# Feed-forward experts of a decoder layer: three batches sorted by expert on chip and computed in tiles of 256 rows, the fourth computed densely

## The chip, the cores and the metric

One core of one Trainium2 chip. The metric is the device time of one execution in microseconds (us); the kernel before has a median of 324.4 us over three runs (324.27 to 324.47).

## The reference, cut to what matters

```python
x = x + self_attention(layernorm(x))                 # B=4, S=256, D=128; 16 heads of 64
x = x + cross_attention(layernorm(x), ctx)           # 16 heads of 8
# the part that changes: x is (4, 256, 128), 8 experts, hidden 512, top 2
n = layernorm(x)
scores = n @ Wr + br
_, topk_idx = top_k(scores, 2)
weights = softmax(where(chosen, scores, -inf))
for i in range(8):
    h = relu((n * chosen[..., i]) @ W1[i] + b1[i])
    out = out + (h @ W2[i] + b2[i]) * weights[..., i]
x = x + out
```

Only 2 of the 8 experts count for a row, so most of a dense evaluation multiplies by a weight of zero.

## The kernel before

The 1024 rows lie as 8 tiles of 128 rows, two per batch. Everything is one launch; each engine gets its instructions from one list of `slots`, made of units such as `("CS", b, g, kt)`, and walks that list in order (TensorE at L953, ScalarE at L1146, VectorE at L1403). GpSimd (POOL) and the DMA queue of SyncE (SP) have hand-written orders of their own (L586 to L629, L423 to L478). Nothing overtakes on an engine; engines meet by semaphores.

The units that matter here, by stage:
- Cross attention of batch b: `CS` (scores, one 128x512 product, L837, then an exponential on ScalarE, L1092), eight pairs per batch; `CO` (16 narrow products, L852); then a chain through bank 7 of PSUM: `oq0`, `oT0`, `oq1`, `oT1`, `wo` (L856 to L872), in which VectorE normalises between `oq` and `oT` (L1328) and ScalarE copies after `oT` (L1103). After `wo` VectorE adds the residual and takes statistics (L1293), and POOL makes the normalised rows (`norm_3`, L561, with `norm_batch`, L546). These steps of batch b lie among the scores of batch b+1. Units that use bank 7 take turns in the order of `misc_at`, each waiting until the one before has been read out.
- Router: `NT` turns the normalised rows (L887), `RT` makes 8 scores per row (L891), `best_two` (L1344) takes the two best, `EX` one exponential, `gates` (L1358) the weights, `WT` turns the weights. It is done in two halves of 512 rows: the first among batch 3's scores, the second within the expert stage.
- Experts: for k = 0 to 15 (expert k % 8, half k // 8 of 512 rows), `X` spreads the weights of expert k over the partitions (L913), VectorE multiplies them onto the rows (`gated`, L1378), and high and low float32r parts are made (`gated_high` L1118 on ScalarE, `gated_low` L1385 on VectorE). For each of four chunks c of 128 hidden columns, `H` is three 128x512 products (`hidden`, L916, through `products`, L661 to L665), read out by ScalarE (`relu_high`, L1123) and VectorE (`relu_low`, L1390), and `Y` three more (`combine`, L934), which add into one PSUM bank over all experts. On TensorE Y of expert k-1 alternates with H of expert k, so each H has a whole expert's worth of chunks before its Y. These are 16 x 4 x 6 = 384 products of 512 columns.
- Weights: POOL subtracts the last row of W1 (`first_weights`, L567) and makes low parts (`first_low` L574, `second_weights` L580); ScalarE makes high parts (`WS`, `W2`).
- The end: `YE` copies the sum, `YO` turns it and VectorE adds it (L1399); four output DMAs (L477).

`resid` holds the running sum of all rows throughout. The first hidden product (k = 0) already waits behind batch 3's last-but-one scores; two of batch 3's score pairs and its whole output chain lie among the first two experts (L294 to L299).

## Time and profile before

| what | value |
|---|---|
| median of the runs | 324.4 us |
| the profiled execution's own time | 326.34 us |
| its span in the trace | 324.6 us |
| mean granted TensorE clock | 0.989 of full speed |
| TensorE matmuls busy | 297.8 us (92%) |
| VectorE, ScalarE busy | 206.5 us (64%), 193.0 us (59%) |
| GpSimd busy | 97.8 us (30%) |

Times in the trace count from the start of the span. A matmul's listed duration runs to the end of its results, and matmuls overlap, so the distance between the starts of two of them is what one costs, not its duration. `PEld` is the loading of weights for the next matmul. SPq, POOLq are the instruction queues: issuing a DMA is not counted as busy. In the waits, `<-` names what ended the idle time.

### The profile page before, as it was taken

How to read it: one execution, taken by the hardware profiler on the slowest of the kernel's cores; microseconds unless marked ns; L12 is line 12 of the kernel's file. 1: busy time of each engine (PE TensorE's matmuls, PEld its weight loads, DVE VectorE, ACT ScalarE, POOL GpSimd, SP SyncE). 2: the span in 40 equal slices, each digit the busy share in tenths (PEclk: the TensorE clock that was granted, in tenths of full speed). 3: DMA queues.
4: the chain of work that ended last, by engine and by line, in shares of the span. 5: the costliest groups of instructions: out<-in, count | busy, mean ns of one | idle time of the engine just before them, and what ended most of it. 6: DMA issues, size and time to landing. Idle time of an engine off the chain costs nothing.

```text
span 324.6 us, 5407 instructions
## 1 busy us (share of the span) xinstructions
PE 297.8 (92%) x1869; PEld 210.2 (65%) x1869; DVE 206.5 (64%) x444; ACT 193.0 (59%) x525; POOL 97.8 (30%) x140
## 2 busy tenths in 40 slices
PE   6789999999989899797989788889999999999995
PEld 2578677877777568453745343436778878678883
DVE  3767657375548885966376673536686867666652
ACT  1569858387747664466276668867655465354451
POOL 7990190035020200720056152055558110000000
PEclk9799999999999999999999999979999999999999
DMA  8900015530100010001084491000000000100001
GB/s 234 210 3 3 1 23 65 67 43 16 36 0 2 16 35 2 5 0 45 5 253 141 112 280 55 3 0 2 0 1 2 0 0 0 35 0 0 2 1 32
DMA packets 14889, 14.06 MB, mean 43 GB/s; under 512 B 2620, under 2 KB 10892, under 8 KB 14860
## 3 DMA queue, kind: packets, MB, share of 16 engines
q1 hardware_dynamic: 13278, 12.92, 16.4%
q10 hardware_dynamic: 1584, 0.80, 0.9%
q8 instruction: 15, 0.25, 0.3%
q14 instruction: 12, 0.10, 0.1%
HBM read 9.94 MB, written 0.52 MB: 32 GB/s over the span
## 4 chain that ended last, share of the span: by engine, by line
PE 73%; DVE 13%; ACT 3%; DMA 3%; issue 3%; SPq 2%; POOL 1%; DVEq 0%; ACTq 0%; POOLq 0%
PE ps L663 7%; PE ps L665 7%; PE ps L664 7%; PE ps L737 6%; PE ps L770 5%; PE ps L782 4%; PE ps L944 4%; PE ps L945 4%; PE ps L946 4%; DVE mneg L1306 4%; PE ps L815 3%; PE ps L852 3%; PE ps L744 2%; SPq L412 2%; DMA w_in<-in_L_attn_W_qkv 2%
## 5 line engine op out<-in xcount | busy, mean ns | idle before, releaser
L1062 ACT ACTIVATE p<-ps,negmax 128x256 f32<-128x256 f32 (+1 forms) x128 | 52.7, 426 | 25.2 <-DVE negmax L1277 24.7
L1392 DVE SCALAR_TENSOR_TENSOR hid_lo<-ps,hid_hi 128x512 fp32r<-128x512 f32 x64 | 43.6, 688 | 33.7 <-ACT hid_hi L1126 33.4
L1306 DVE TENSOR_REDUCE mneg<-ps 128x2 f32<-128x512 f32 x64 | 42.5, 684 | 18.6 <-PE ps L815 18.5
L1126 ACT ACTIVATE hid_hi<-ps 128x512 fp32r<-128x512 f32 x64 | 37.5, 598 | 26.8 <-PE ps L665 26.7
L1092 ACT ACTIVATE px<-ps 128x512 f32<-128x512 f32 x64 | 36.1, 598 | 17.8 <-PE ps L837 17.5
L1277 DVE TENSOR_REDUCE negmax<-ps 128x2 f32<-128x512 f32 (+1 forms) x48 | 32.9, 686 | 19.6 <-PE ps L739 12.5
L815 PE MATMUL ps<-k_st,q_mem 128*128 128x256 bf16 x128 | 24.7, 276 | 9.0 <-DVE mneg L1306 7.6
L504 POOL TENSOR_SCALAR tmp<-mv 128x2 f32<-128x2 f32 x8 | 1.9, 233 | 95.3 <-DVE mv L1301 95.3
L1048 ACT CAST t_hi<-ps 128x512 fp32r<-128x512 f32 x32 | 18.8, 592 | 19.5 <-PE ps L665 18.6
L663 PE MATMUL ps<-x_hi,w_hi 128*128 128x512 f32 x64 | 25.6, 400 | 1.7 <-issue 1.5
L1062 ACT ACTIVATION_READ_ACCUMULATOR p<-ps,negmax 128x1 f32 x128 | 26.6, 208 | 0.0
L944 PE MATMUL ps<-hid_hi,w_hi 128*128 128x512 f32 x64 | 25.9, 404 | 0.0
L665 PE MATMUL ps<-x_lo,w_hi 128*128 128x512 f32 x64 | 25.5, 398 | 0.0
L837 PE MATMUL ps<-q_mem,k_st 128*128 128x512 bf16 x64 | 23.6, 389 | 2.0 <-DMA q_mem<-m_part 1.1
L945 PE MATMUL ps<-hid_hi,w_lo 128*128 128x512 f32 x64 | 25.3, 395 | 0.0
L946 PE MATMUL ps<-hid_lo,w_hi 128*128 128x512 f32 x64 | 25.2, 395 | 0.0
L664 PE MATMUL ps<-x_hi,w_lo 128*128 128x512 f32 x64 | 25.2, 394 | 0.0
L737 PE MATMUL ps<-t_hi,n_parts 128*128 128x512 f32 x64 | 23.1, 442 | 0.3 <-DVE t_lo L1243 0.3
L815 PEld LDWEIGHTS ps<-k_st,q_mem 128*128 128x128 bf16 x128 | 9.1, 97 | 21.9 <-DVE mneg L1306 15.3
L1243 DVE TENSOR_TENSOR t_lo<-ps,t_hi 128x512 fp32r<-128x512 f32 x32 | 21.4, 681 | 2.5 <-ACT t_hi L1048 2.5
L1121 ACT CAST x_hi<-x_f 128x512 fp32r<-128x512 f32 x16 | 9.9, 620 | 21.2 <-DVE x_f L1382 21.1
L663 PE MATMUL ps<-n_parts,g_hi 128*128 128x256 f32 x64 | 20.6, 322 | 0.0
(184 smaller groups left out, 663.7 us busy)
## 6 DMA issues: line engine op xcount, KB each, us to landing
w_raw<-in_L_ffn_W SPq DMA_DIRECT2D x2, 1024.0 KB, 6.1
w_last<-in_L_ffn_W SPq DMA_DIRECT2D x8, 256.0 KB, 6.1
k_st<-k_part SPq DMA_DIRECT2D x12, 128.0 KB
q_mem<-q_part SPq DMA_DIRECT2D x48, 32.0 KB
w_in<-in_L_attn_W_qkv ACTq DMA_DIRECT2D x2, 384.0 KB, 6.3
w_in<-in_L_attn_W_qkv SPq DMA_DIRECT2D x2, 384.0 KB, 7.1
resid<-in_x SPq DMA_DIRECT2D x2, 256.0 KB, 4.0
p<-in_L_attn_W_o SPq DMA_DIRECT2D x1, 512.0 KB, 8.3
```

Of the source, the lines that this page charges most:

```text
L663: pe.matmul(out, a[0], b_[0], start=True, stop=False)
L664: pe.matmul(out, a[1], b_[0], start=False, stop=False)
L665: return pe.matmul(out, a[0], b_[1], start=False, stop=True)
L737: pe.matmul(bank, n_parts[:, a, S * b:S * b + P], t_ring[t][:, 2 * (u % 6):2 * (u % 6) + 2, :], start=(a + t == 0), stop=False)
L815: last = pe.matmul(ps[:, max_bank[("MX", b, u)], S * par:S * par + S], q_st[b][:, g, S * par + P * qt:S * par + P * qt + P], k_st[:, g, S ...
L944: pe.matmul(bank, w[0], h[0], start=(e == 0 and c == 0), stop=False)
L945: pe.matmul(bank, w[1], h[0], start=False, stop=False)
L946: pe.matmul(bank, w[0], h[1], start=False, stop=(e == NE - 1 and c == NC - 1)).then_inc(s_y, 1)
L1062: last = act.activation(dst, bank[:, n * i:n * i + n], ACT.Exp, bias=negmax[:, kt, h:h + 1], accum_out=psums[:, kt, h:h + 1])
L1126: act.activation(hid[0][:, c, :], ps[:, hidden_banks[NC * k + c], :], ACT.Relu).then_inc(s_ha, 1)
L1306: dve.tensor_reduce(mneg[:, qt, :].rearrange("p (r g) -> p r g", r=2)[:, :, g], ps[:, max_bank[("MX", b, u)], :].rearrange("p (h k) -> p h ...
L1392: dve.scalar_tensor_tensor(hid[1][:, c, :], ps[:, hidden_banks[NC * k + c], :], 0.0, hid[0][:, c, :].bitcast(F32), ALU.max, ALU.subtract). ...
```

## The change

What it does:
- Batches 0 to 2 (6 tiles, 768 rows, so 1536 row-and-expert pairs) are routed in two groups, `ROUTED` 0 (tiles 0 to 3) and 1 (tiles 4 and 5). For each, `PS` counts on TensorE how many earlier pairs went to the same expert (`ranks`, with triangular and all-ones matrices), and VectorE makes a place from that (`places`, 12 steps ahead of `s_pos`, each waiting for the one before; 6 more behind it for the first group). POOL then scatters the rows to a buffer in HBM (`dispatch`, an indirect DMA for each tile and choice: 8 for group 0, 4 for group 1; each 128 rows of 528 bytes).
- The buffer has 13 places of 256 rows: one for each of 8 experts, 5 spares for what overflows. All 13 are computed, filled or not. Three loads bring them back (`xr`), then SP copies the weights of each spare's expert within the chip (`spare_weights`, four DMAs of 256 KB, five times).
- The expert stage is now 13 sorted tiles ("S") and then the 8 experts on batch 3's 256 rows ("D"): 21 units of 256 rows, each of two halves u with 6 products of H and 6 of Y, all of 256 columns: 504 products. S tiles are turned (`rows_in`), split, computed, given their bias on ScalarE (`tile_out`), turned back (`YT`), copied (`rows_out`) and scattered by POOL to HBM (`collect`, two indirect DMAs a tile, 26 in all). D tiles are multiplied by their weights as before.
- `CB` adds the collected rows times their weights for batches 0 to 2 during D's last units; their output leaves before the last batch's.
- The list of slots: batch 3's scores and its whole output chain now lie ahead of the expert stage. In it, batch 2's chain comes a half to one slot sooner. The weight copies `WS` move up into batch 1 and 2.
- POOL's order: weights, norm_3(0), norm_3(1), four `second_weights`, 8 dispatches, norm_3(2), 4 dispatches, two `second_weights`, norm_3(3), two more, 26 collects. Before the stage it also builds tables; the buffer is filled by one DMA in batch 0.

```diff
+DT, ST = TPB, NT - TPB
+PAIRS = 2 * ST * P
+CAP = 256
+SPARE = PAIRS // (CAP + 1)
+NS = NE + SPARE
+ROW = D + 4
+
+ORDER = tuple(range(NE // 2)) + tuple(j for i in range(SPARE) for j in ((NE + i, NE // 2 + i) if i < NE // 2 else (NE + i,)))
+SEQ = tuple([("S", j) for j in range(NS)] + [("D", e) for e in range(NE)])
+
+ROUTED = ((0, 2 * TPB), (2 * TPB, ST), (ST, NT))
...
+            for g, unit in zip(((0, 0, 1, 2, 3, 5.5, 6.5), (1.5, 2.5, 3, 4.5, 5.5), (0.5, 1.5, 2, 3, 3.5), (0.5, 1, 1.5, 2, 2.5))[b], units):
...
-            more = {(1, 6): [("WS", 0, 0)], (2, 1): [("WS", 0, 1)], (2, 5): [("WS", 0, 2)], (2, 6): [("NT", 0)],
-                    (2, 7): [("RT", 0)], (3, 0): [("EX", 0)], (3, 0.5): [("GT", 0)], (3, 2): [("W2", 0, 0)],
-                    (3, 3): [("WT", 0), ("WS", 0, 3)], (3, 4): [("X", 0)]}
+            more = {(1, 4): [("WS", 0, 0)], (1, 5): [("WS", 0, 1)], (1, 6): [("WS", 0, 2)],
+                    (1, 7): [("WS", 0, 3), ("BT", 0)], (2, 0): [("WS", 0, 4)], (2, 1): [("WS", 0, 5)],
+                    (2, 2): [("WS", 0, 6)], (2, 3): [("WS", 0, 7)], (2, 4): [("XC", 0)], (2, 5): [("W2", 0, 0)],
+                    (2, 7): [("W2", 0, 1)], (3, -0.5): [("NT", 0)], (3, 0): [("RT", 0), ("XC", 1)],
+                    (3, 1): [("W2", 0, 2)], (3, 2): [("PS", 0)], (3, 3): [("W2", 0, 3)], (3, 4): [("NT", 1)],
+                    (3, 5): [("RT", 1), ("XC", 2)], (3, 6): [("W2", 0, 4)], (3, 6.5): [("PS", 1)]}
...
+        slots.append([("CO", last, 3), ("oq0", last), ("oT0", last), ("W2", 0, 5), ("oq1", last), ("oT1", last),
+                      ("wo", last), ("W2", 0, 6), ("OV", 0)])
+        beside = {(0, 1, "h"): [("W2", 0, 7)], (2, 0, "h"): [("NT", 2)], (2, 1, "h"): [("RT", 2)],
+                  (3, 0, "h"): [("EX", 0)], (3, 1, "h"): [("GS", 0), ("EX", 1)], (4, 0, "h"): [("EX", 2)],
+                  (4, 1, "h"): [("GT", 0)], (5, 1, "h"): [("WT", 0), ("GS", 1)],
+                  (NS + 6, 0, "h"): [("CB", 0)], (NS + 6, 1, "h"): [("CB", 1)], (NS + 7, 0, "h"): [("CB", 2)]}
...
+            slot = [("X", x) for x, tiles in enumerate(x_units) if x == i == 0 or x and tiles[0] == i + 1]
+            for u in range(2):
+                if i:
+                    slot += [("Y", i - 1, u)]
+                    kind, j = SEQ[i - 1]
+                    if u == 1 and kind == "S":
+                        slot += [("E", j)]
+                    if u == 0 and i >= 2 and SEQ[i - 2][0] == "S":
+                        slot += [("YT", SEQ[i - 2][1])]
+                slot += beside.get((i, u, "y"), [])
+                if i < len(SEQ):
+                    slot += [("H", i, u)]
+                slot += beside.get((i, u, "h"), [])
...
+            sp.wait_ge(s_xs, 16 * 2 * ST)
+            for i, (n0, n1) in enumerate(XR_PARTS):
+                sp.dma_start(xr[:, 2 * n0:2 * n1, :], xs.rearrange("(n p) d -> p n d", p=P)[:, 2 * n0:2 * n1, :]
+                             ).then_inc(s_xr[i], 16)
+
+            def spare_weights(o):
+
+                if o >= 2:
+                    sp.wait_ge(s_y, 2 * SEQ.index(("S", ORDER.index(NE + o - 2))) + 2)
+                e = sp.value_load(spare_i[0:1, o:o + 1], min_val=0, max_val=NE - 1)
+                for k, w in enumerate((w1_hi, w1_lo, w2_hi, w2_lo)):
+                    sp.dma_start(ovw[:, o % 2, k, :].bitcast(F32), w[:, bass.ds(e * HID, HID)].bitcast(F32)
+                                 ).then_inc(s_ovw[o % 2], 16)
...
+            def dispatch(t, c):
+
+                pool.wait_ge(s_pos, 1 if t < ROUTED[0][1] else 2)
+                pool.wait_ge(s_n3, t + 1) if c == 0 else pool.wait_ge(s_copied, t // TPB + 1)
+                pool.indirect_dma_start(xs, bass.IndirectOffsetOnAxis(pos_i[:, t, c:c + 1], 0),
+                                        xrow[:, t, c, :], None).then_inc(s_xs, 16)
+
+            def collect(j):
+
+                pool.wait_ge(s_misc_ev, misc_at[("YT", j)] + 1)
+                for h in range(2):
+                    pool.indirect_dma_start(ys, bass.IndirectOffsetOnAxis(xr[:, 2 * ORDER[j] + h, D:D + 1].bitcast(U32), 0),
+                                            yrow[:, j % 2, P * h:P * h + P], None, bounds_check=PAIRS - 1,
+                                            oob_is_err=False).then_inc(s_ys[j % 2], 16)
...
-            for i in range(3):
+            for i in range(6):
                 first_weights(i)
+            first_low(0)
+            first_weights(6)
+            first_low(1)
+            first_weights(7)
+            first_low(2)
+            first_low(3)
             norm_3(0)
-            first_low(0)
-            first_weights(3)
-            first_weights(4)
+            first_low(4)
+            first_low(5)
+            first_low(6)
             norm_3(1)
-
-            pool.wait_ge(s_xlo, 1)
-            first_low(1)
-            second_weights(0)
-            first_low(2)
-            for i in range(5, NE):
-                first_weights(i)
+            first_low(7)
+            for i in range(4):
+                second_weights(i)
+            pool.wait_ge(s_init, 16)
+            for t in range(ROUTED[0][1]):
+                for c in range(2):
+                    dispatch(t, c)
             norm_3(2)
-            first_low(3)
-            second_weights(1)
-            second_weights(2)
+            for t in range(*ROUTED[1]):
+                for c in range(2):
+                    dispatch(t, c)
+            second_weights(4)
+            second_weights(5)
             norm_3(3)
-            for i in range(4, NE):
-                first_low(i)
-                second_weights(i - 1)
-            second_weights(NE - 1)
+            second_weights(6)
+            second_weights(7)
+            for j in range(NS):
+                collect(j)
...
+            def ranks(g):
+                one = hots[g]
+                n = one.shape[1] - 1
+                if g == 0:
+                else:
+                    pe.wait_ge(s_rank_ev, g)
+                pe.wait_ge(s_tab, 9)
+                pe.wait_ge(s_hot, 2 * g + 1)
+                count = ps[:, R_BANK, 0:NE * (n + 1)].rearrange("p (j e) -> p j e", e=NE)
+                pe.matmul(count, below[:, :], one[:, :, :], start=True, stop=False)
+                if g == 1:
+                    pe.wait_ge(s_hot, 2)
+                    pe.matmul(count, ones[:, :], seen[:, :].unsqueeze(1).to_broadcast([P, n + 1, NE]), start=False, stop=False)
+                for j in range(n):
+                    last = pe.matmul(count[:, j + 1:n + 1, :], ones[:, :], one[:, j:j + 1, :].to_broadcast([P, n - j, NE]),
+                                     start=False, stop=(j == n - 1))
+                last.then_inc(s_rank, 1)
...
+            def hidden(i, u):
...
+                for n in range(2):
+                    c = slice(P * (2 * u + n), P * (2 * u + n) + P)
+                    if kind == "D" or j < NE:
+                        w = [w[:, j, c] for w in w1_p]
+                    else:
+                        w = [ovw[:, j % 2, k, c] for k in range(2)]
+                    last = products(ps[:, bank, CAP * n:CAP * n + CAP], w,
+                                    [part[:, x % 2, CAP * half_x:CAP * half_x + CAP] for part in x_p])
+                last.then_inc(s_h, 1)
...
+            def combine(i, u):
...
+                if at == 0 and u == 0:
+                    pe.wait_ge(s_pv_ev, last_in(Y_BANK[kind], ((m, out_bank(m)) for m in range(2 * B))) + 1)
+                elif kind == "S" and u == 0:
+                    pe.wait_ge(s_yev, at)
+                pe.wait_ge(s_hd, 2 * i + u + 1)
+                opens = u == 0 and (kind == "S" or j == 0)
+                closes = u == 1 and (kind == "S" or j == NE - 1)
+                for n in range(2):
+                    c = 2 * u + n
+                    if kind == "D" or j < NE:
+                        w = [w[:, NC * j + c, :] for w in w2_p]
+                    else:
+                        w = [ovw[:, j % 2, 2 + k, P * c:P * c + P] for k in range(2)]
+                    h = [part[:, (2 * i + u) % NC, CAP * n:CAP * n + CAP] for part in hid]
+                    pe.matmul(bank, w[0], h[0], start=(opens and n == 0), stop=False)
+                    pe.matmul(bank, w[1], h[0], start=False, stop=False)
+                    last = pe.matmul(bank, w[0], h[1], start=False, stop=(closes and n == 1))
+                last.then_inc(s_y, 1)
...
+                step(dve.tensor_copy(top_f[:, ts, :], top_i[:, ts, 0:2]))
+                if n < 2:
+                    both = 2 * (t1 - t0)
+                    dve.wait_ge(s_tab, 9)
+                    dve.tensor_tensor(hots[n][:, 0:both, :], iota8[:, :].unsqueeze(1).to_broadcast([P, both, NE]),
+                                      top_f[:, ts, :].rearrange("p t c -> p (t c)").unsqueeze(2).to_broadcast([P, both, NE]),
+                                      ALU.is_equal).then_inc(s_hot, 1)
+                    dve.wait_ge(s_hot, 2 * n + 1)
+                if n == 0:
+                    step(dve.tensor_reduce(seen_f[:, :], hots[0][:, 0:both, :].rearrange("p j e -> p e j"), AX, ALU.add))
+                    dve.tensor_copy(seen[:, :], seen_f[:, :]).then_inc(s_hot, 1)
...
+            def places(g):
...
+                if g == 0:
+                    step(dve.tensor_scalar(now, count[:, n, :], float(CAP), None, ALU.is_gt))
+                else:
+                    step(dve.tensor_tensor(now, count[:, n, :], edge[:, :], ALU.is_gt))
+                step(dve.tensor_tensor(prod8[:, :, :], lower[:, :, :], now.unsqueeze(1).to_broadcast([P, NE, NE]), ALU.mult))
+                step(dve.tensor_reduce(before, prod8[:, :, :], AX, ALU.add))
+                if g == 0:
+                    step(dve.tensor_scalar(full[:, :], before, float(CAP), float(CAP * (NE - 1)), ALU.mult, ALU.add))
+                    step(dve.tensor_tensor(delta, full[:, :], tile0[:, :], ALU.subtract))
+                    step(dve.tensor_scalar(passed[:, 0:n, :], count[:, 0:n, :], float(CAP), None, ALU.is_gt))
+                    begin = tile0[:, :]
+                else:
+                    step(dve.scalar_tensor_tensor(prod8[:, 0, :], before, float(CAP), full[:, :], ALU.mult, ALU.add))
+                    step(dve.tensor_tensor(delta, prod8[:, 0, :], base[:, :], ALU.subtract))
+                    step(dve.tensor_tensor(passed[:, 0:n, :], count[:, 0:n, :], by_pair(edge[:, :]), ALU.is_gt))
+                    begin = base[:, :]
+                step(dve.tensor_tensor(passed[:, 0:n, :], passed[:, 0:n, :], by_pair(delta), ALU.mult))
+                dve.tensor_tensor(place[:, 0:n, :], count[:, 0:n, :], by_pair(begin), ALU.add).then_inc(s_rank_ev, 1)
+                dve.wait_ge(s_rank_ev, g + 1)
+                step(dve.tensor_tensor(place[:, 0:n, :], place[:, 0:n, :], passed[:, 0:n, :], ALU.add))
+                step(dve.tensor_tensor(place[:, 0:n, :], place[:, 0:n, :], one[:, 0:n, :], ALU.mult))
+                step(dve.tensor_reduce(slot_f[:, 0:n], place[:, 0:n, :], AX, ALU.add))
+                t0, t1 = ROUTED[g]
+                dve.tensor_scalar(pos_i[:, t0:t1, :].rearrange("p t c -> p (t c)"), slot_f[:, 0:n], -1.0, None,
+                                  ALU.add).then_inc(s_pos, 1)
...
+            def gated(x):
+                n = x_kind[:x].count("D")
+                dve.wait_ge(s_gt, x + 1)
+                if n >= 2:
+                    dve.wait_ge(s_xhi, [k for k in range(x) if x_kind[k] == "D"][n - 2] + 1)
+                dve.tensor_tensor(x_f[:, n % 2, :].rearrange("p (e q) -> p e q", e=2),
+                                  ps[:, X_BANK, :].rearrange("p (e q) -> p e q", e=2),
+                                  nT[:, ST * P:NT * P].unsqueeze(1).to_broadcast([P, 2, CAP]), ALU.mult).then_inc(s_xf, 1)
+            def rows_low(x):
+                dve.wait_ge(s_xhi, x + 1)
+                cols = slice(0, CAP * len(x_units[x]))
+                src = x_f[:, x_kind[:x].count("D") % 2, :] if x_kind[x] == "D" else ps[:, X_BANK, :]
+                dve.tensor_tensor(x_p[1][:, x % 2, cols], src[:, cols], x_p[0][:, x % 2, cols].bitcast(F32), ALU.subtract
+            def relu_low(i, u):
+                n = 2 * i + u
+                dve.wait_ge(s_ha, n + 1)
+                dve.scalar_tensor_tensor(hid[1][:, n % NC, :], ps[:, hidden_banks[n], :], 0.0,
+                                         hid[0][:, n % NC, :].bitcast(F32), ALU.max, ALU.subtract).then_inc(s_hd, 1)
+            def rows_out(j):
+                dve.wait_ge(s_misc, misc_at[("YT", j)] + 1)
+                ge(dve, s_ys[j % 2], 32 * (j // 2))
+                dve.tensor_copy(yrow[:, j % 2, :], ps[:, 7, 0:CAP]).then_inc(s_misc_ev, 1)
```

## Rows read from the trace of the kernel before

**Rows 1.** The page, the chain that ended last, by engine

```profile
PE 73%; DVE 13%; ACT 3%; DMA 3%; issue 3%; SPq 2%; POOL 1%; DVEq 0%; ACTq 0%; POOLq 0%
```

**Rows 2.** Windows: us, then PE, PEld, DVE, ACT, POOL busy, granted clock, DMA

```profile
187.00:204.00 17.00, 15.17 (x128) 7.36 (x128) 9.51 (x28) 12.16 (x26) 6.05 (x10) 1.00 0.55 153
204.00:214.00 10.00, 7.77 (x72) 3.55 (x71) 5.32 (x32) 8.92 (x18) 0.00 (x0) 1.00 0.01 2
214.00:219.00 5.00, 4.36 (x24) 1.97 (x25) 1.83 (x3) 2.52 (x6) 4.38 (x4) 0.66 0.00 0
219.00:320.00 101.00, 99.84 (x456) 78.67 (x456) 68.48 (x135) 53.56 (x101) 23.45 (x27) 1.00 0.01 3
```

**Rows 3.** Timeline: start, length, engine; last batch's scores, first and last expert products

```profile
203.52 0.59 PE L837 MATMUL ps<-q_mem,k_st 128*128 128x512 bf16 x2
...
214.64 0.47 PE L663 MATMUL ps<-x_hi,w_hi 128*128 128x512 f32 x1 [1.52 <-issue]
...
319.93 0.39 PE L946 MATMUL ps<-hid_lo,w_hi 128*128 128x512 f32 x1
```

**Rows 4.** Timeline of TensorE: neighbouring products of 512 and of 256 columns, transposes

```profile
296.05 0.39 PE L944 MATMUL ps<-hid_hi,w_hi 128*128 128x512 f32 x1
...
297.20 0.39 PE L665 MATMUL ps<-x_lo,w_hi 128*128 128x512 f32 x1
```

```profile
100.03 0.28 PE L664 MATMUL ps<-n_parts,g_lo 128*128 128x256 f32 x1
...
100.50 0.29 PE L665 MATMUL ps<-n_parts,g_hi 128*128 128x256 f32 x1
```

```profile
208.62 0.60 PE L862 MATMUL ps<-ident,o_raw 128*128 128x128 f32 x4
```

**Rows 5.** Timeline: one hidden chunk read out, and the rows of one expert made

```profile
314.37 0.39 PE L665 MATMUL ps<-x_lo,w_hi 128*128 128x512 f32 x1
...
314.80 0.60 ACT L1126 ACTIVATE hid_hi<-ps 128x512 fp32r<-128x512 f32 x1 [0.80 <-PE ps L665]
...
315.44 0.69 DVE L1392 SCALAR_TENSOR_TENSOR hid_lo<-ps,hid_hi 128x512 fp32r<-128x512 f32 x1 [0.71 <-ACT hid_hi L1126]
```

```profile
301.66 0.68 DVE L1382 TENSOR_TENSOR x_f<-ps,nT 128x512 f32<-128x512 f32 x1
...
302.37 0.62 ACT L1121 CAST x_hi<-x_f 128x512 fp32r<-128x512 f32 x1 [1.35 <-DVE x_f L1382]
```

**Rows 6.** Timeline of VectorE: the first half's two best, and a normalisation

```profile
203.70 0.19 DVE L1348 COPY score<-ps 128x32 f32<-128x32 f32 x1 [5.09 <-PE ps L891]
...
205.43 0.17 DVE L1356 TENSOR_TENSOR gate<-top 128x4 f32<-128x4 f32 x1
...
207.45 0.18 DVE L1374 CAST wgt_p<-wgt 128x32 fp32r<-128x32 f32 x1
...
208.06 0.35 DVE L1335 TENSOR_TENSOR o_n<-ps,r_den 128x64 f32<-128x64 f32 x2
```

**Rows 7.** Timeline of GpSimd: the normalised rows of one batch

```profile
198.78 0.23 POOL L504 TENSOR_SCALAR tmp<-mv 128x2 f32<-128x2 f32 x1 [7.82 <-DVE mv L1301]
...
200.24 0.91 POOL L551 TENSOR_SCALAR norm<-resid,negm,rstd 128x127 f32<-128x127 f32 x2
```

**Rows 8.** All instructions of two lines: ns min/median/max, first and last start

```profile
L577 POOL TENSOR_TENSOR w_lo<-w_raw,w_hi x8: 1267/1292/1725, 187.2 to 250.0; 128x512 fp32r<-128x512 f32 x8
L1387 DVE TENSOR_TENSOR x_lo<-x_f,x_hi x16: 679/681/1530, 213.8 to 309.9; 128x512 fp32r<-128x512 f32 x16
```

**Rows 9.** The queue of SP: twelve issues in a row, the slowest single issue

```profile
172.07 7.88 SPq L412 DMA_DIRECT2D q_mem<-q_part  x12
...
3.84 3.10 SPq L387 DMA_DIRECT2D wx<-in_L_xattn_Wq  x1
```

**Rows 10.** DMA issues: count, KB each, median us from issue to landing

```profile
w_last<-in_L_ffn_W SPq DMA_DIRECT2D x8, 256.0 KB, 6.1
out_dram<-resid SPq DMA_DIRECT2D x4, 128.0 KB, 1.9
```

More of the change, by code:

```diff
@@ L300, in decoder_layer @@
[L300 to L312 removed]
+                slots.append(slot)
@@ L453, in _ @@
             first_experts(0)
-            for i in range(LAST_RING):
+            stack_m(1)
+            for i in range(LAST_HALF, NE):
                 last_rows(i)
-            stack_m(1)
             first_experts(1)
@@ L893, in expert_step @@
                 elif kind == "WT":
[L894 to L902 removed]
+                    pe.wait_ge(s_wgt, 1)
```

534 lines of the change are left out of this document (334 added, 200 removed).

## The prediction

> **What bounds the kernel now.** I read the chain of waits by engine first: TensorE carries 73% of it, no other engine over 13% [rows 1]. The windows show where: from 219 to 320 us TensorE is busy 99.84 of 101.00 us at the full clock (2.4 GHz), VectorE 68.48 and ScalarE 53.56, both with room [rows 2]. That is the expert stage; its first product starts at 214.64 and its last at 319.93 [rows 3]. Ahead of it batch 3's scores start at 203.52 [rows 3], and TensorE still works 7.77 of 10 us there [rows 2]. So two numbers decide: when the first hidden product starts, and how long the stage takes from there. Behind the last product's start come 4.7 us to the end of the span of 324.6 us.
>
> **TensorE's saving.** Five starts lie between the products at 296.05 and 297.20, 0.23 us each for 512 columns; four between 100.03 and 100.50, 0.1175 each for 256 [rows 4]. Before: 384 x 0.23 = 88.3 us and 16 weight spreads, 3.7. After: 21 units x 24 = 504 products x 0.1175 = 59.2 us. So 29 us go, a third and not three quarters: 13 tiles of 256 rows stand for 24 (8 experts on 768 rows), filled or not. Added are 26 transposes in and 26 out; four take 0.60 with the last one's own tail, 0.115 each [rows 4], 6.0 us. The dense spreads (0.9) and batch 3's turns, router and bias (1.3) make TensorE's floor 67.4 us.
>
> **Waits inside the new loop.** Before, a chunk had four chunks' time to be read out. Now H(i,0) is followed by Y(i-1,1) and H(i,1), 1.41 us, and then Y(i,0) needs it. The relay: last product issued at 314.37, ScalarE at 314.80 for 0.60, VectorE from 315.44 for 0.69, done at 316.13 [rows 5]. With 256 columns the product is 0.11 shorter (0.28 against 0.39 [rows 4]): 1.7 us with the step back to TensorE, against 1.41 + 0.12. I take 0.25 per unit, with one weight load laid bare: 5.3 us; the ends are 0, if turns lie between, and 0.5. Every second dense unit first makes its rows: VectorE 0.68, ScalarE 0.62 [rows 5], VectorE 0.68 again, with the next chunk's read-out queued behind them on both engines, so Y comes 1.3 us late: 4 x 1.3 = 5. The third group's best two and weights sit in VectorE's queue in units 2 to 5 (some 25 steps of 0.2, worked out below): 2.5 us beyond its room. The last Y finds no H to cover it: 0.9. The stage now opens after an idle TensorE; before, 1.52 us idle [rows 3] were followed by a mean clock of 0.66 from 214 to 219 [rows 2], about 2 us lost; again 2. Sum 15.7; the stage takes 67.4 + 15.7 = 83.1 us from first to last product issue. Before it took 105.3.
>
> **When it starts.** This is where the change pays. The steps, from the anchor at 203.52 [rows 3]:
> - ScalarE has 12.16 of 17 us busy from 187 to 204 [rows 2] and gets some five more weight copies of 0.6: 1 us late, scores at 204.5 (ends 0 and 3, the whole 3 us of copies).
> - Turn, copy, CO and router products: done at 207.5. VectorE's best two took 1.73 (203.70 to 205.43), short dependent steps 0.20 each (ten from 205.43 to 207.45) [rows 6]. Five more steps for the counts: 210.4. Batch 2's normalisation is queued behind them, and `oT0` behind that stalls TensorE 2.5 us. After the two halves of that chain `PS` counts until 214.5. `places` has 12 steps of up to 0.24: 217.4. POOL's fourth `second_weights` needs ScalarE's copy in slot (3,3), which TensorE reaches only then: POOL is free at 218.4.
> - Eight dispatches. No row shows an indirect DMA. Below, an issue on SP takes 0.65 (7.88 for twelve); above, the slowest issue took 3.10 [rows 9]. POOL must work through 128 rows itself, like its own pass over 128x512, 1.29 [rows 8], so I take 1.2, the nearest row: 9.6 us, until 228.0.
> - norm_3(2) is queued behind them: 2.4 us (198.78 to 200.24 + 0.91 [rows 7]), 230.4. `NT(1)` in slot (3,4) waits for it on TensorE, with the rest of batch 3's scores behind it. TensorE has been idle since about 217 and returns at 1.2 GHz.
> - Turn, copy, router 2.0; best two for two tiles 1.9; counts 0.8; places 2.8: 237.9.
> - Four dispatches 4.8: 242.8. Landing in HBM 1.9 as an output DMA; then SP's issue 0.5 and the load of 270 KB, between 1.9 and 6.1 [rows 10]; small and alone, 2.5: 247.7.
> - Turns at half clock 1.1, high part 0.6, low part 0.7, handovers 0.2: first hidden product at **250.3**, 35.7 us later than before. Batch 3's output chain (some 9 us of products that overlapped experts before) fits into these waits and costs nothing; without the cover it would cost its 9 us.
>
> What else moves costs nothing while this chain is the longest: SP's fill of the buffer and four more row loads go out early in batch 0, where SP waits anyway; POOL's tables lie in its idle time; the first spare's weights (four 256 KB copies, 6.1 each at most [rows 10], overlapping) start near 249 and are needed at tile 4, near 266. Collects take 2 x 1.2 of the 3.5 us of a tile and are off the chain below 1.7 us each. Batches 0 to 2's output DMAs are out before the last, which stays.
>
> **The Trainium skill beside the dispatches.** Their issue is taken at 1.2 us from rows of other operations [rows 8, 9]. "DMA: Bandwidth & Descriptors", section "Latency and other measured facts", puts the first byte of a DMA issued by GpSimd at about 1 us, for descriptors written by software; by it, as an estimate of the issue, 12 dispatches would cost 12.0 and not 14.4, and the sum would be 335.3.
>
> **Sum.** 250.3 + 83.1 + 4.5 (the end, one copy shorter) = 337.9 us of span, 13.3 over the profiled execution's 324.6. That execution's own time was 326.34, the median of the runs is 324.4, 0.2 under its span; I carry the span's difference over to the median: 324.4 + 13.3 = 337.7.
>
> **The rivals.**
> - *The loop hides its relay and the scatter is cheap: faster.* VectorE and ScalarE have room [rows 2], and weight loads and turns may fill the 0.2 us gaps. Then 5.3, 5 and 2.5 of the waits go (12.8), and at 0.65 a dispatch 12 x 0.55 = 6.6 more: 337.7 - 19.4 = 318.3. It decides when the first product starts before 237 with my loop, or before 250 with a loop free of those waits. Against it: two trips through HBM and two VectorE chains that no row lets shrink. 0.17.
> - *The scatter is dear.* At 1.7 us each the collects fill a tile, and `rows_out` on VectorE waits for the scatter two tiles back, with the hidden read-outs behind it. At 2.0: 12 x 0.8 + 13 x 0.5 = 16, 354; at 3.10, 12 x 1.9 + 13 x 2.7 = 58, 396. 0.13 for over 350.
> - *POOL and VectorE hold each other up.* POOL's 1.29 us pass took up to 1.73, VectorE's 0.68 us subtraction of two on-chip operands up to 1.53 [rows 8], at times when both ran. If each dispatch on the path meets this, 12 x 0.44 = 5.3: 343. 0.12. The Trainium skill, "SBUF — State Buffer", section "SBUF: two separate sides", says that GpSimd and VectorE share one port pair under an exclusive lock, and that descriptor writing by GpSimd is shut out meanwhile; by that rule, the 1.73 and 1.53 agree.
> - *It doesn't save what it says.* Fixed tiles mean that no routing makes it shorter; were full tiles of 256 columns no cheaper than 0.14 each, 504 products would cost 11 us more, 349. It is part of the forecast's chance, near its upper end.
>
> **Chances.** The forecast, with values from 328 to 350: 0.50. The lock 0.12, dear scatter 0.13, between 325 and 328 0.05: slower by over 0.2% together 0.80. Faster 0.17. Within 0.2%, about what a measurement of this kernel can tell from no change, 0.03. The range reaches down into the fast case, to 321, and up to 353: it leaves out the fastest 0.1 and the dearest 0.1.
>
> **What would show it.** In the changed kernel's profile: 504 products 0.12 apart; TensorE idle for 10 us or more ahead of `NT(1)` and again ahead of the first hidden product; that product near 250; a granted clock at half when it opens; in VectorE's waits the hidden low part on ScalarE, in TensorE's the second product on VectorE; dispatch issues 1.2 us apart on POOL. I am wrong if the first product starts before 240 us, or the stage takes under 75 us.

## The result and the profile after

The changed kernel takes **336.1 us** (median of 4 runs, 335.84 to 336.61) against 324.3 us before (4 runs, 324.14 to 324.47): 1.0365 times as long, 95% interval 1.0347 to 1.0383. Forecast were 337.7 us, range 321 to 353. The profiled execution's own time is 336.61 us, its span 334.9.

The chain of the page, by engine, answers to [rows 1]: TensorE falls from 73% to 57%, and what comes in is VectorE, "issue", POOL and DMA.

```profile
PE 57%; DVE 18%; issue 9%; DMA 5%; POOL 5%; ACT 3%; SPq 3%; POOLq 0%; ACTq 0%; DVEq 0%
```

The windows (columns as in [rows 2]) say where. Up to 214 us nothing much has changed. From 219 to 231 TensorE does 0.19 us of work and its granted clock falls to 0.50; from 237 to 249 it works 4.85 of 12 us, and the clock falls again. Only then the stage runs.

```profile
214.00:219.00 5.00, 2.96 (x24) 1.56 (x23) 4.42 (x19) 3.16 (x6) 2.14 (x2) 0.88 0.00 0
219.00:225.00 6.00, 0.00 (x0) 0.00 (x0) 1.06 (x5) 0.00 (x0) 4.48 (x6) 0.75 0.14 45
225.00:231.00 6.00, 0.19 (x1) 0.22 (x2) 0.00 (x0) 0.00 (x0) 4.71 (x8) 0.50 0.14 45
...
237.00:243.00 6.00, 3.15 (x26) 1.58 (x26) 2.80 (x15) 1.53 (x4) 3.02 (x3) 0.96 0.07 25
243.00:249.00 6.00, 1.70 (x8) 1.43 (x8) 3.82 (x16) 0.79 (x2) 5.56 (x9) 0.50 0.50 138
249.00:255.00 6.00, 4.55 (x21) 4.18 (x21) 1.75 (x3) 2.18 (x4) 1.29 (x2) 0.50 0.71 179
```

```profile
251.00:331.00 80.00, 73.31 (x570) 70.30 (x570) 48.44 (x106) 37.38 (x71) 26.66 (x27) 0.97 0.29 97
```

The timeline of TensorE (start, length, engine, idle time before it and what ended it) has the four waits. It answers to [rows 3]: the last batch's scores as before, 203.58 against 203.52, the first hidden product at 251.07 against 214.64, 36.4 us later. Its last product is issued at 330.87, so the stage takes 79.8 us against 105.3.

```profile
203.58 0.39 PE L973 MATMUL ps<-q_mem,k_st 128*128 128x512 bf16 x1 [1.66 <-DMA q_mem<-m_part]
...
230.81 0.66 PE L1018 MATMUL ps<-ident,xrow 128*128 128x128 f32 x2 [13.59 <-POOL xrow L643]
...
248.53 1.09 PE L1081 MATMUL ps<-ident,xr 128*128 128x128 f32 x4 [3.95 <-DMA xr<-xs]
...
251.07 0.55 PE L799 MATMUL ps<-x_hi,w_hi 128*128 128x256 f32 x1 [1.45 <-issue]
...
330.87 0.28 PE L1137 MATMUL ps<-hid_lo,w_hi 128*128 128x256 f32 x1
```

The timeline of POOL shows what TensorE waited for in the 13.59 us ahead of `NT(1)`: its fourth low part, eight dispatches, then the normalisation of batch 2, whose scaling at 229.76 releases `NT(1)`. Two neighbouring dispatches start 1.26 us apart: 0.96 of work and 0.30 between.

```profile
216.68 1.27 POOL L678 TENSOR_TENSOR w_lo<-w_raw,w_hi 128x512 fp32r<-128x512 f32 x1 [4.20 <-ACT w_hi L1308]
218.13 1.24 POOL L685 DMA_INDIRECT xs<-xrow,pos_i  x1 [0.18 <-issue]
...
222.22 0.96 POOL L685 DMA_INDIRECT xs<-xrow,pos_i  x1 [0.31 <-issue]
223.48 0.96 POOL L685 DMA_INDIRECT xs<-xrow,pos_i  x1 [0.30 <-issue]
...
229.76 0.91 POOL L643 TENSOR_SCALAR xrow<-resid,negm,rstd 128x127 f32<-128x127 f32 x2
239.13 1.10 POOL L685 DMA_INDIRECT xs<-xrow,pos_i  x1 [8.46 <-DVE pos_i L1657]
```

In the stage (waits of TensorE from 251 to 332 us: line, what ended it, us in total, times, longest) the longest item is eight waits of second products for the hidden low part. TensorE is idle for 80.00 - 73.31 = 6.7 us in that window.

```profile
PE ps L1135 <- DVE hid_lo L1705: 5.3, 8, 1.1
PE ps L1030 <- DVE yrow L1711: 0.8, 1, 0.8
```

That idle time is less than what the waits cost. It counts from the end of the product before (0.28 us behind its start), while the next product could have started 0.12 behind it, and the product after a stop comes 0.20 and not 0.12 later. So each stop costs 0.24 us more than the trace lists, and a short one isn't listed at all:

```profile
281.04 0.28 PE L801 MATMUL ps<-x_lo,w_hi 128*128 128x256 f32 x1
281.41 0.36 PE L1135 MATMUL ps<-hid_hi,w_hi 128*128 128x256 f32 x1
281.60 0.28 PE L1136 MATMUL ps<-hid_hi,w_lo 128*128 128x256 f32 x1
```

Added up by the distances between starts, the stops of the stage cost 9.8 us: the nine listed ones and five short ones of this kind (at 258.41, 281.41, 288.28, 324.58 and 326.38).

### The profile page after: what moved, and what is told of

Read it like the earlier page. It is cut to its first block, busy times and chain, and to the rows that moved or that the text cites. A ratio compares the mean times of both kernels' runs of the same rounds, so it can differ in the third digit from the quotient of the medians.

```text
span 334.9 us, 5929 instructions
## 1 busy us (share of the span) xinstructions
PE 279.0 (83%) x2035; PEld 206.1 (62%) x2035; DVE 197.3 (59%) x471; ACT 184.1 (55%) x513; POOL 136.4 (41%) x188
## 4 chain that ended last, share of the span: by engine, by line
PE 57%; DVE 18%; issue 9%; DMA 5%; POOL 5%; ACT 3%; SPq 3%; POOLq 0%; ACTq 0%; DVEq 0%
PE ps L873 6%; PE ps L799 5%; PE ps L800 5%; PE ps L801 5%; PE ps L906 5%; PE ps L918 4%; PE ps L951 4%; DVE mneg L1534 3%; PE ps L988 3%; PE ps L1135 3%; POOL xs L685 3%; PE ps L880 2%; SPq L478 2%; PE ps L1137 2%; DVE hid_lo L1705 2%
## 5 line engine op out<-in xcount | busy, mean ns | idle before, releaser
L1505 DVE TENSOR_REDUCE negmax<-ps 128x2 f32<-128x512 f32 (+1 forms) x48 | 32.9, 686 | 19.6 <-PE ps L875 12.4
L1705 DVE SCALAR_TENSOR_TENSOR hid_lo<-ps,hid_hi 128x512 fp32r<-128x512 f32 x42 | 28.6, 689 | 25.7 <-ACT hid_hi L1327 25.6
L1327 ACT ACTIVATE hid_hi<-ps 128x512 fp32r<-128x512 f32 x42 | 25.1, 598 | 33.7 <-PE ps L801 33.6
L692 POOL DMA_INDIRECT ys<-yrow,xr x26 | 25.4, 976 | 27.5 <-DVE yrow L1711 21.3
L973 PE MATMUL ps<-q_mem,k_st 128*128 128x512 bf16 x64 | 24.7, 405 | 2.1 <-DMA q_mem<-m_part 1.7
L1135 PE MATMUL ps<-hid_hi,w_hi 128*128 128x256 f32 x64 | 19.8, 309 | 4.8 <-DVE hid_lo L1705 4.3
L988 PE MATMUL ps<-px,v_pad 128*32 128x256 f32 x256 | 19.4, 426 | 1.9 <-ACT px L1284 1.1
L799 PE MATMUL ps<-x_hi,w_hi 128*128 128x256 f32 x64 | 19.4, 304 | 1.4 <-issue 1.4
L906 PE MATMUL ps<-p,v_sb 128*64 128x256 f32 x128 | 20.1, 392 | 0.0
L800 PE MATMUL ps<-x_hi,w_lo 128*128 128x256 f32 x64 | 18.6, 290 | 0.0
L801 PE MATMUL ps<-x_lo,w_hi 128*128 128x256 f32 x64 | 18.4, 288 | 0.0
```

Source lines behind the costliest of these rows:

```text
L799: pe.matmul(out, a[0], b_[0], start=True, stop=False)
L800: pe.matmul(out, a[1], b_[0], start=False, stop=False)
L801: return pe.matmul(out, a[0], b_[1], start=False, stop=True)
L906: last = pe.matmul(o, v, p0[:, h, :], start=True, stop=False)
L1135: pe.matmul(bank, w[0], h[0], start=(opens and n == 0), stop=False)
L1505: dve.tensor_reduce(dst, ps[:, k % 3, :].rearrange("p (h q) -> p h q", h=n), AX, ALU.max, negate=True).then_inc(s_max, 1)
```

## The experiments

Each kernel is the changed one with the edit shown. The runs of the kernel before that went with them had medians of 324.9 us (`norm_early`, `late_y`, `no_cb`, `no_gate`), 324.7 (`two_more`, `both`, `both_w2`, `warm`) and 324.8 (`ps_early`, `last`), spread wider than in the first measurement (324.0 to 327.3), so ratios are to these. The changed kernel was not run again: a difference to its 336.1 us compares two measurements, between which the kernel before moved by 0.4 to 0.6 us. Measured against the kernel before, each saving is larger, and the loss of `two_more` smaller, by that much.

**norm_early.** One part of POOL's order.

```diff
             for t in range(ROUTED[0][1]):
                 for c in range(2):
                     dispatch(t, c)
-            norm_3(2)
+                if t == 0:
+                    norm_3(2)
```

> Batch 2's third normalisation stands on POOL between the second and the third dispatch of group 0 instead of behind the eighth. Theory A (the chain through POOL sets the start of the stage, and the stage is as long whenever it starts): six dispatches of 1.26 us less ahead of NT(1), which comes at 230.8 - 7 = 224 us instead of 230.81; the first hidden product at 244 instead of 251.07, the time 329.2, 6.9 less. Theory B (the start isn't what bounds the end: collects on POOL, the spare weights or VectorE's queue do): first product earlier, time down by under 3 us. Theory C (the eight dispatches themselves then end later than group 1's places and hold its own dispatches): NT(1) 7 us earlier but first product by under 4.

Measured 329.3 us, 1.014 times before (1.0073 to 1.0207), so 6.8 less than the changed kernel. TensorE's timeline: `NT(1)` at 224.06, first hidden product at 243.53.

```profile
224.06 0.66 PE L1019 MATMUL ps<-ident,xrow 128*128 128x128 f32 x2 [6.75 <-POOL xrow L643]
...
241.00 1.09 PE L1082 MATMUL ps<-ident,xr 128*128 128x128 f32 x4 [3.81 <-DMA xr<-xs]
...
243.53 0.55 PE L800 MATMUL ps<-x_hi,w_hi 128*128 128x256 f32 x1 [1.44 <-issue]
```

Theory A (that the median agrees to the tenth is partly luck: the four runs go from 327.8 to 331.5): what comes out of the chain ahead of `NT(1)` comes out of the time, and neither collects nor spare weights take its place. The stage is as long as before (79.5 us from first to last product). POOL's dispatches now run on without a pause until 236.5, so POOL alone is the chain.

**two_more.** The same chain made longer.

```diff
                 for c in range(2):
                     dispatch(t, c)
+            for c in range(2):
+                pool.indirect_dma_start(xs_2, bass.IndirectOffsetOnAxis(pos_i[:, 3, c:c + 1], 0),
+                                        xrow[:, 3, c, :], None).then_inc(s_xs, 16)
             norm_3(2)
```

The load of the rows waits for these two as well.

> Two dispatches more behind group 0's eight: batch 1's second tile is scattered once more, into an array of its own that nobody reads. Theory A (each dispatch ahead of NT(1) stands in the chain with its spacing of 1.26 us): 2.5 us more, 338.6, with NT(1) at 233.3. Rival (what bounds is the landing of the rows or VectorE, and POOL's issue fills its waits): under 1 us more.

Measured 339.7 us, 1.0455 times before (1.041 to 1.050), 3.6 more. In its trace `NT(1)` comes at 233.54 (2.7 later), the first hidden product at 253.95 (2.9 later), the span is 338.1, 3.2 longer. Theory A holds: from the first dispatch to `NT(1)` it takes 15.21 us instead of 12.68, 2.53 more, which is two spacings. Of the rest over 2.5, about 0.4 is the difference between the two measurements, and 0.2 stands ahead of the first dispatch; what is left is not explained.

**late_y.** The stage's own waits, by a change of order: `H(i,u)` now stands ahead of `Y(i-1,u)` and not behind it.

```diff
             for u in range(2):
+                if i < len(SEQ):
+                    slot += [("H", i, u)]
                 if i:
                     slot += [("Y", i - 1, u)]
...
-                if i < len(SEQ):
-                    slot += [("H", i, u)]
```

> Each second product stands behind one more hidden product on TensorE, so that ScalarE and VectorE have 2.1 us of TensorE's work and not 1.4 for the read-out of a hidden chunk. TensorE was idle for some 6.6 us of the stage between 255 and 331 us. Theory A (the read-out relay is what TensorE waits for, and the rows of the dense units through it): 5 to 6 us less, some 330.5, and the waits of the second product on the hidden low part (5.3 us) go to under 1. Theory B (the gaps are VectorE's or POOL's load and come back elsewhere, at the turns or the next rows): under 2 us less.

Measured 330.6 us, 1.0166 times before (1.0115 to 1.0217), 5.6 less. Waits of TensorE in its stage, and the window of the stage:

```profile
PE ps L1134 <- DVE hid_lo L1704: 1.2, 2, 0.9
PE ps L1029 <- DVE yrow L1710: 0.7, 1, 0.7
PE ps L1017 <- DVE yrow L1710: 0.7, 1, 0.7
```

```profile
251.40:325.00 73.60, 71.02 (x570) 69.54 (x570) 48.34 (x106) 37.86 (x72) 26.67 (x27) 0.97 0.32 105
```

The wait on the hidden low part falls from 5.3 us to 1.2 (the last `Y`, 0.86, and one behind the additions of `CB`, 0.33). From the first product at 251.37 to the last at 324.67 the stage takes 73.3 us, 6.5 less. VectorE does the same work as before in it (48.34 against 48.44), so its total load was not the bound: only the distance between a hidden chunk and its use was too short. By the distances between starts the stops of the stage cost 3.6 us here instead of 9.8. The 1.2 us are a little over what was expected.

**no_cb.** The additions of `CB` left out: `dve.sem_inc(s_sum, 1)` stands in place of each.

> Leaves out the sums of batches 0 to 2 (the gated rows added to the residual), so their output lacks the experts' part; the loads of those rows stay. The twelve additions take 3.76 us of VectorE between 324.35 and 329.39 us, where hidden read-outs stand behind them. Theory A (they stand in the read-out relay of the last three dense units, but fill gaps for most of it): 1 to 2 us less. Theory B (VectorE is the bound of the last units): the whole 3.8 us. Theory C (nothing waits for them): within 0.3 us.

Measured 335.4 us, 1.0338 times before (1.0281 to 1.0395): 0.7 less, under the 1 to 2 expected. TensorE's waits on the hidden low part are 4.5 us in 7 instead of 5.3 in 8:

```profile
PE ps L1135 <- DVE hid_lo L1705: 4.5, 7, 1.0
```

The wait at 328.37 (0.31) is gone and that of the last `Y` falls from 0.86 to 0.38. So of 3.76 us of VectorE's work about 1 was paid, and the rest lay in gaps. (From first product to the end the profile is 2.1 us shorter, of which 1.0 is a clock that came back 2 us sooner, so the profile and the median bracket 0.7 to 1.1. The medians alone can't show it: one of the four runs, 337.5, is slower than all of the changed kernel's.)

**no_gate.** The rows of three of the four dense pairs not made:

```diff
                 dve.wait_ge(s_gt, x + 1)
+                if n >= 1:
+                    dve.sem_inc(s_xf, 1)
+                    return
```

(Not shown: the high and the low part then read the first pair's rows.)

> The last three of the four dense row pairs aren't made: VectorE's multiplication of batch 3's rows by their weights is left out there, and the first pair's rows are used again, so batch 3's output is weighted otherwise. What stays is the high part on ScalarE and the low part on VectorE. TensorE stood still for 1.06, 0.57, 0.93 and 0.31 us at the four pairs. Theory A (the read-outs queue behind the making of the rows, VectorE 0.69 us each): 3 x 0.3 to 3 x 0.7, 1 to 2 us less. Theory B (the pair's 2 x 0.69 + 0.6 us lie in gaps): within 0.3 us.

Measured 335.1 us, 1.0297 times before (1.0249 to 1.0346): 1.0 less. The waits on the hidden low part fall to 2.7 us in 5.

```profile
PE ps L1135 <- DVE hid_lo L1708: 2.7, 5, 1.0
```

The expectation has the waits wrong by one place. The four pairs' rows are made at 296.23, 303.95, 311.44 and 318.60, and the waits behind them are 1.04 (at 299.36), 1.06, 0.57 and 0.93 us; the 0.31 at 328.37 belongs to `CB`. The edit leaves the first of them (1.01 here) and takes away the other three, 2.6 us, half of the listed wait.

```profile
299.36 0.36 PE L1135 MATMUL ps<-hid_hi,ovw 128*128 128x256 f32 x1 [1.04 <-DVE hid_lo L1705]
```

In their place three short stops of the relay stay, with starts 0.36 to 0.37 apart, so that from the first pair's wait to the one at `CB` the trace is 2.3 us shorter (26.74 against 29.01). The median gained only 1.0: the runs of this kernel spread from 334.1 to 336.4, and in the profiled one the first hidden product came at 253.30, 2.2 later than in the changed kernel, for reasons ahead of anything that the edit touches (0.7 of it is the held step of the last section). For the stage the trace decides, for the whole time the medians don't.

**both.** `norm_early` and `late_y` together.

> Batch 2's normalisation between the second and the third dispatch, and each second product one hidden product later, together. Theory A (the start of the stage and its length are independent terms): 6.9 and 5.5 us less together, 323.7, which is the time of the kernel before. Theory B (both gains draw on the same slack, for instance POOL's collects or the spare weights now bound the stage): 3 us or more above that.

Measured 323.6 us, 0.9956 times before (0.9928 to 0.9984): the two terms add up, 6.8 + 5.6 = 12.4 against 12.5. Theory A. With two changes of order the sorted kernel is level with the one before.

**both_w2.** POOL's fourth low part to a place where nobody waits for it.

```diff
-            for i in range(4):
+            for i in range(3):
                 second_weights(i)
...
+            second_weights(3)
             second_weights(4)
             second_weights(5)
```

> As the last, and POOL's fourth low part of the second weights, which waits for ScalarE (POOL L678, 4.20 us of wait and 1.27 of work up to 217.95 us), moved behind the last dispatch of group 1. Theory A (POOL's chain from its last work before the dispatches to group 1's last dispatch sets the start): the dispatches start when places(0) is done, 216.9 instead of 218.13, 1.2 us less than the last kernel, 322.4. Rival (places(1) or the output chain of the last batch takes over): under 0.4 us less.

Measured 322.3 us, 0.9913 times before (0.9881 to 0.9945): 1.3 less than `both`, though the two intervals overlap. POOL's timeline has the first dispatch at 217.38 (218.77 in `both`, of which 0.7 is the held step of the last section) and the twelfth at 234.39, with one short wait for VectorE: both chains now end nearly together. The first dispatch is 0.5 later than expected: it starts 0.86 us behind the step of VectorE that it waits for (216.52).

```profile
217.38 1.24 POOL L684 DMA_INDIRECT xs<-xrow,pos_i  x1 [5.82 <-issue]
...
230.60 0.95 POOL L684 DMA_INDIRECT xs<-xrow,pos_i  x1 [0.65 <-DVE pos_i L1658]
...
234.39 0.96 POOL L684 DMA_INDIRECT xs<-xrow,pos_i  x1 [0.30 <-issue]
```

**warm.** `both_w2`, with products on TensorE that nobody reads.

```diff
+            def keep_busy(bank, n):
+                for _ in range(n):
+                    pe.matmul(ps[:, bank, :], ident_b[:, :], mask[:, :, :], start=True, stop=True)
...
+                if (kind, n) == ("NT", 1):
+                    keep_busy(6, 24)
...
                 if x == 0:
+                    keep_busy(4, 8)
                     pe.wait_ge(s_mx_ev, 16 * B)
...
                 last.then_inc(s_gt, 1)
+                if x == 0:
+                    keep_busy(4, 4)
```

> As the last, and TensorE works in its waits: 24 products of 512 columns that nobody reads ahead of NT(1), 8 ahead of the first rows' turns and 4 behind them. The granted clock was 0.50 (1.2 GHz) from 225 to 231 us and again for some 4.5 us behind the first hidden product. Theory A (the idle stretches cost the clock at the opening of the stage, half of 4.5 us and half of the turns' 1.1): 2 to 2.5 us less than the last kernel, 320.1, with hidden products 0.12 us apart from the first on. Rival (the clock falls all the same, or the products that nobody reads hold the work up): no gain, or up to 1.5 us more.

Measured 320.5 us, 0.9853 times before (0.9814 to 0.9891), 1.8 less than `both_w2`; but "0.12 us apart from the first on" is a miss. TensorE's timeline: the eight products end at 238.2, 2.16 us of waiting follow, and the first hidden products come 0.21 apart, at the lower level of 1.2 GHz.

```profile
234.85 3.33 PE L1015 MATMUL ps<-mask,ident_b 128*128 128x512 bf16 x8
240.34 0.63 PE L1090 MATMUL ps<-ident,xr 128*128 128x128 f32 x4 [2.16 <-DMA xr<-xs]
...
243.07 0.41 PE L801 MATMUL ps<-x_hi,w_lo 128*128 128x256 f32 x1
243.29 0.41 PE L802 MATMUL ps<-x_lo,w_hi 128*128 128x256 f32 x1
```

The half clock lasts 1.9 us behind the first hidden product (to 244.6) instead of 5.0 (251.07 to 256.1 in the changed kernel; 5.0 in `both_w2` too), so the expected sum was nearly right and its place was not.

**ps_early.** `warm`, and group 0's places ahead of everything that VectorE doesn't owe them.

```diff
-                    (3, 1): [("W2", 0, 2)], (3, 2): [("PS", 0)], (3, 3): [("W2", 0, 3)], (3, 4): [("NT", 1)],
+                    (3, 1): [("W2", 0, 2)], (3, 0.5): [("PS", 0)], (3, 2.5): [("PT", 0)], (3, 3): [("W2", 0, 3)], (3, 4): [("NT", 1)],
...
-                if t == 0:
+                if t == 1:
                     norm_3(2)
...
-                    keep_busy(6, 24)
+                    keep_busy(6, 14)
...
-                if g == 0:
+            def edges():
+                    now, delta = over[:, 0, :], shift[:, 0, :]
```

(`edges` holds the last six steps of places(0), and `PT` calls it.)

> The last kernel (warm) with the counts of group 0 ahead of `oT0` in slot (3,1) on TensorE instead of in slot (3,2), places(0) following on VectorE, its last six steps (for group 1's edges) put behind batch 2's residual; the normalisation of batch 2 behind the fourth dispatch, and 14 idle products instead of 24 ahead of NT(1). The hots are done at 209.3 us in the changed kernel and the counts came at 213.9. Theory A (VectorE's places(0) and POOL's chain set the start): dispatches begin at about 213.5 instead of 217.4 to 218.3, group 1's places become the bound at 228.3, its last dispatch ends 2 us earlier, 318.4. Rival (VectorE's queue is the bound: oq1's normalisation and the residual behind places(0) come later by what the dispatches gain): within 0.5 us of warm, 320.5.

Measured **317.8 us, 0.978 times before** (0.9744 to 0.9816), 2.7 less than `warm` where 2.1 were expected. The first dispatch starts at 214.20, and POOL now waits 1.48 us for group 1's places, as foreseen. The first hidden product comes at 239.81, and at the full clock: TensorE waited only 0.93 us ahead of the first turns. (The clock was 0.50 from 232.4 to 235.8 and back before the turns.) Windows of this kernel:

```profile
233.00:239.00 6.00, 4.79 (x19) 2.22 (x18) 4.81 (x16) 0.59 (x1) 5.61 (x10) 0.77 0.65 178
239.00:245.00 6.00, 5.19 (x44) 5.22 (x45) 3.68 (x7) 3.51 (x7) 2.82 (x3) 1.00 0.50 127
```

**last.** The wait ahead of the first turns filled as well: `keep_busy(4, 15)` and `(4, 6)`.

> As ps_early, with 15 products that nobody reads instead of 8 ahead of the first rows' turns and 6 instead of 4 behind them. In warm TensorE stood idle for 2.16 us ahead of these turns and the granted clock was 0.50 again from 242 to 244.2 us. Theory A (with that stretch filled the first turns and hidden products run at the full clock): the turns 0.4 us and the first hidden products 0.9 us shorter, 1.0 us less than ps_early, 317.4. Rival (the clock falls all the same, or the added products end later than the rows land): within 0.3 us, or more.

Measured 318.6 us, 0.9805 times before (0.976 to 0.9849): no gain over `ps_early` (its runs, 316.9 to 321.2, cover those of `ps_early`). `ps_early` opened at the full clock by itself, so there was no clock left to win, and the rival came true: the products that nobody reads end later than the rows land. The load of the first rows, issued at 235.01, landed 3.1 us later, at 238.1. TensorE was still at its added products, at half the clock (until 238.9), and came to the turns at 239.82.

```profile
234.74 5.25 PE L1015 MATMUL ps<-mask,ident_b 128*128 128x512 bf16 x14 [0.22 <-issue]
239.82 0.60 PE L1090 MATMUL ps<-ident,xr 128*128 128x128 f32 x4
```

The first hidden product starts at 241.87 instead of 239.81; of these 2.1 us, 0.7 stand already ahead of the first dispatch (214.86 for 214.20). The window shows the clock:

```profile
233.00:239.00 6.00, 5.48 (x15) 2.66 (x17) 4.10 (x13) 0.76 (x2) 5.65 (x8) 0.51 0.58 156
```

## Why the prediction was right, step by step

Right in sign and within 1.6 us, with 336.1 for 337.7, and for the reason given, though the closeness is partly luck (see the end of this section): the stage got 25.5 us shorter (forecast 22.2) and started 36.4 us later (35.7), and `norm_early` and `two_more` show that the late start is POOL's chain. The steps:

- **Scores 1 us late: wrong.** 203.58; the five weight copies of ScalarE (14.13 of 17 us busy against 12.16) were free. From there the next three steps ran 0.6 to 1.1 us ahead of the forecast: hots at 209.3, counts at 213.9, places at 216.7 (210.4, 214.5, 217.4).
- **POOL free at 218.4: right.** 218.13, and by the wait named, ScalarE's copy in slot (3,3). `both_w2` took it away.
- **A dispatch 1.2 us: right**, 1.26. Eight ended at 228.2 (228.0), the normalisation at 230.7 (230.4), `NT(1)` at 230.81. The estimate came from POOL's 128x512 pass of 1.29; that it fits so well is partly luck, since a dispatch is made up otherwise, of 0.96 us of work and 0.30 between two. By the Trainium skill, "DMA: Bandwidth & Descriptors", section "Latency and other measured facts", about 1 us was to be expected for the first byte; the trace has 0.96 of work, but 1.26 from one to the next, and it is the spacing that adds up.
- **Group 1 to the first hidden product: right in sum.** Places 238.9 (237.9), twelfth dispatch done 244.0 (242.8), its rows landed 1.4 behind that (1.9), the load of 264 KB 3.0 with its issue (0.5 + 2.5), turns at 248.53 (247.7), first product 251.07 (250.3). From `NT(1)` to there it took 20.3 us, forecast were 19.9.
- **TensorE's saving: right.** The products stand 0.117 to 0.118 us apart. The rival of costly full tiles is out.
- **Waits in the loop: right in kind; the relay's term was too big.** Forecast were 13.7 us together: 5.3 for the relay, 5 for the dense rows, 2.5 for group 3's routing in VectorE's queue and 0.9 for the last `Y`. By the distances between starts the trace has 9.8. By its parts:
  - The dense pairs 4.5 (starts 1.32, 1.34, 0.85 and 1.21 apart and not 0.12, and 0.07 more for the product behind): nearly right.
  - Group 3's routing 2.0 (the stops at 266.30, 273.86 and 274.55): nearly right.
  - The last `Y` 1.1: nearly right.
  - The relay 1.7 and not 5.3. This is the one mis-sized term. A stop has the size forecast, 0.25 us and a weight load laid bare (0.08), but only five stand by themselves in 21 units. In every second sorted unit four turns lie ahead of `Y` and hide it, the lower end that the forecast named (0), among the dense units the spreading of two experts' weights does so, and elsewhere it is part of a longer wait.
  - 0.5 behind `CB`, at 328.37, for which nothing was put down.
- **TensorE's floor: right.** With 67.4 for it, 2.5 for the clock (below) and 9.8 for the stops, 79.7 of the stage's 79.8 us are accounted for. The turns held too: four cost 0.36 us and 0.08 for the weight load behind them, 0.11 each where 0.115 stood.
- **CB: not in the forecast.** 3.76 us of VectorE's work behind which the last read-outs queue; it cost 0.7 to 1.1.
- **Clock: right.** 2 us were put down; the first 5.0 us of the stage ran at 0.50, which costs half of it, 2.5.
- **The lock as a rival: wrong in its place.** No dispatch grew: 0.95 to 0.97 us throughout, 1.10 to 1.24 for the first of a row. VectorE's steps did, and in some runs one that the dispatches wait for (below).
- **The fast rival** asked for a first product before 237, or before 250 with a loop free of waits. Neither came of itself; `ps_early` comes near to both (239.81, no relay), and its 317.8 us is near the 318.3 worked out for that case, by another way: POOL's order and not cheaper dispatches.
- **Luck in the sum.** The stage was 3.3 us shorter than forecast and started 0.8 later, and the end took 0.5 less: the span was 334.9 where 337.9 was forecast, 3.0 off. The medians are only 1.6 off, because the forecast carried a difference of spans over to the median, and the profiled execution of the kernel before lay further above its median (326.34 for 324.4) than that of the changed kernel (336.61 for 336.1).

## What to carry to other kernels

A queue that issues work for several consumers should serve the one that opens the longest chain first: six dispatches ahead of one small normalisation cost 6.8 us here. When a loop's units get shorter, the distance between producing and using an intermediate must grow with the relay (2.1 us of TensorE's work instead of 1.4 paid 5.6 us, with no engine working less). What such waits cost is read from the distances between starts: here the listed idle time, 6.7 us, left out a third of 9.8. A kernel that saves a third of its matmuls can still lose by the trip that sorts the rows; read the gain against the delay of the stage's first product before anything else, and then look at whether the delay is transfer or mere order.

## What the runs showed of the hardware that was not expected

**A VectorE step can be held until a POOL pass ends.** In the changed kernel one step on 8 columns, like its neighbours of 0.17 us, took 1.14: it starts at 216.83, POOL's pass L678 runs from 216.68 to 217.95, and the step ends at 217.97. Timeline of VectorE:

```profile
216.64 0.16 DVE L1661 TENSOR_TENSOR base<-over,shift 128x8 f32<-128x8 f32 x1
216.83 1.14 DVE L1662 TENSOR_TENSOR base<-base,tile 128x8 f32<-128x8 f32 x1
218.01 0.17 DVE L1663 TENSOR_SCALAR edge<-over 128x8 f32<-128x8 f32 x1
```

In `both_w2`, where this POOL pass stands elsewhere, no step of places(0) is stretched; the step that took 1.14 there:

```profile
216.62 0.17 DVE L1663 TENSOR_TENSOR base<-base,tile 128x8 f32<-128x8 f32 x1
```

In `ps_early` places(0) falls together with another POOL pass (211.27 to 212.53), and the step begun at 211.65 takes 0.97 and ends at 212.62, 0.1 behind it. So the stretched one ends where the pass ends, and it can lose to the next pass too: the step begun at 235.02 in `ps_early`, in the second of three passes in a row (233.02 to 236.73), took 1.75 us, until the third had ended. In `norm_early`, `late_y`, `no_cb`, `no_gate` and `both` the held step is the one that writes `pos_i` (0.87 to 1.09 us instead of 0.17), and the first dispatch waits for it. It starts 0.9 us behind the end of the pass there (in `norm_early` 218.94 behind 218.04) and 0.18 behind it in the changed kernel, where `pos_i` was ready: 0.7 us on the path. It is not each step in the pass that suffers: in `ps_early` the one begun at 211.39, which reads `ps`, took 0.23, and the statistics of a batch beside the later passes kept their 0.18 to 0.29. The Trainium skill, "SBUF — State Buffer", section "SBUF: two separate sides", says that the two engines share a port pair under an exclusive lock; the trace agrees. Both steps with two operands in SBUF (`base` and a table) and with one (`slot_f`) were held; which operations ask for it, these rows don't tell. The VectorE steps beside the dispatches kept their 0.15 to 0.17 us.

**Short waits can cost the clock as well as long ones.** In `ps_early` no wait of TensorE between 223.7 and 232.5 is longer than 0.94 us, but they follow one another in the last batch's output chain (0.94, 0.80, 0.74, 0.36, 0.74), and the granted clock was 0.50 from 232.4 to 235.8; it was 1.00 again while the added products ran, and a wait of 0.93 us ahead of the turns left it there. In `warm` the clock was back at 1.00 from 237.7. TensorE ran until 238.2 and stood idle for 2.16 us, and the clock fell to 0.50 again at 241.2, when TensorE was already at work again. In `last` TensorE had no wait behind 234.74, and the clock, at 0.50 since 232.1, still stayed there until 238.9. The way back took 5.0 us of work behind the first hidden product in the changed kernel and 3.0 in `no_cb`.
